# Second expert layer: two of eight token tiles through all eight experts instead of sorted blocks

## The reference, cut to what matters

```python
logits = xt @ Wg.T                                   # 1024 x 8
topk_logits, topk_idx = jax.lax.top_k(logits, TOP_K) # TOP_K = 2
w = jax.nn.softmax(topk_logits, axis=-1)
gates = jnp.zeros((T, N_EXPERTS), xt.dtype).at[rows, topk_idx].add(w)
h = jnp.einsum('th,ehi->tei', xt, W1) + b1           # 128 -> 512 for each expert
h = jax.nn.gelu(h, approximate=False)
o = jnp.einsum('tei,eih->teh', h, W2) + b2           # 512 -> 128
y = jnp.einsum('te,teh->th', gates, o)
x = _layernorm(x + y)
```

## Time and profile before

| | |
|---|---|
| median of 3 runs | 872.15 us (870.58 to 873.14) |
| the profiled execution | 871.81 us, of which the span in the profile is 870.0 us |
| mean granted clock of PE | 0.863 of full |
| PE busy | 706.4 us (81%) |
| DVE busy | 587.0 us (67%) |
| ACT busy | 452.8 us (52%) |
| POOL busy | 441.5 us (51%) |

### The profile page before, as it was taken

How to read it: one execution, slowest core, us unless ns; L and a number is a source line. 1 busy time by engine, 2 the same in 40 slices (tenths; PEclk the granted TensorE clock), 3 DMA queues, 4 the chain that set the end, 5 groups by cost and what they waited for, 6 DMA issues and landing times.

```text
span 870.0 us, 21282 instructions
## 1 busy us (share of the span) xinstructions
PE 706.4 (81%) x7894; PEld 524.7 (60%) x7894; DVE 587.0 (67%) x1552; ACT 452.8 (52%) x1155; POOL 441.5 (51%) x595
## 2 busy tenths in 40 slices
PE   5997987899989996999958998649968999733990
PEld 2575754667867784777526776316545667532980
DVE  4657859899889865798478987403348889541544
ACT  2214646677887654777516764304426767311660
POOL 3119835676656632443246874124556667342452
PEclk9658978899999998999978998659969999755995
DMA  8009200000000000000038000030026570003012
GB/s 325 5 9 293 35 2 1 1 1 2 2 1 1 2 2 1 3 3 3 2 12 280 3 3 2 4 91 32 35 67 182 168 210 3 3 28 92 32 37 76
DMA packets 50803, 44.66 MB, mean 51 GB/s; under 512 B 15408, under 2 KB 41136, under 8 KB 50192
## 3 DMA queue, kind: packets, MB, share of 16 engines
q1 hardware_dynamic: 48464, 38.70, 16.0%
q0 software_dynamic: 2240, 4.60, 1.5%
HBM read 30.94 MB, written 12.36 MB: 50 GB/s over the span
## 4 chain that ended last, share of the span: by engine, by line
PE 48%; DVE 16%; issue 16%; POOL 6%; ACT 5%; DMA 5%; SPq 2%; DVEq 0%; POOLq 0%; ACTq 0%
PE bank L830 4%; PE bank L809 4%; PE bank L818 3%; PE bank L989 3%; PE bank L1062 3%; PE bank L1055 2%; PE bank L727 2%; PE bank L899 2%; PE bank L845 2%; DMA rel_scratch<-G 2%; DVE pairs L1570 2%; DVE pairs L1566 2%; PE bank L876 2%; PE bank L720 1%; PE bank L740 1%
## 5 line engine op out<-in xcount | busy, mean ns | idle before, releaser
L1880 POOL TENSOR_TENSOR sm<-sm,mx 128x512 f32<-128x512 f32 x80 | 83.8, 1049 | 41.9 <-DVE mx L1520 41.3
L1851 POOL TENSOR_SCALAR veps<-mv 128x1 f32<-128x1 f32 x112 | 26.9, 240 | 117.7 <-DVE mv L1455 117.5
L1153 ACT COPY pT<-bank 128x512 f32<-128x512 f32 x112 | 65.4, 584 | 36.4 <-PE bank L818 35.0
L1148 ACT ACTIVATE pr<-sm 128x512 f32<-128x512 f32 x112 | 70.1, 632 | 25.4 <-POOL sm L1880 24.6
L818 PE MATMUL bank<-W,pr 128*128 128x128 f32 x448 | 71.6, 283 | 7.5 <-ACT pT L1153 6.0
L1875 POOL TENSOR_TENSOR pairs<-KS,quad 128x512 f32<-128x512 f32 x56 | 59.9, 1071 | 35.1 <-ACT KS L1130 35.0
L1852 POOL TENSOR_TENSOR rstd<-veps,W 128x1 f32<-128x1 f32 x112 | 65.1, 581 | 9.3
L830 PEld LDWEIGHTS bank<-VX,pT 64*64 64x64 f32 x3584 | 60.2, 139 | 13.5 <-issue 7.6
L809 PE MATMUL bank<-pairs,Q 64*128 64x256 f32 x448 | 66.3, 415 | 2.0 <-DVE sm L1505 1.0
L830 PE MATMUL bank<-VX,pT 64*64 64x9 f32 (+1 forms) x3584 | 65.4, 203 | 2.9 <-ACT pT L1153 1.2
L818 PEld LDWEIGHTS bank<-W,pr 128*128 128x128 f32 x448 | 50.4, 143 | 19.4 <-issue 10.9
(11 more groups left out here) (344 smaller groups left out, 1909.5 us busy)
## 6 DMA issues: line engine op xcount, KB each, us to landing
big<-gup SPq DMA_DIRECT2D x4, 1024.0 KB, 10.0
rel_scratch<-G SPq DMA_DIRECT2D x16, 256.0 KB, 2.8
W<-small SPq DMA_DIRECT2D x1, 3206.5 KB, 12.4
big<-early SPq DMA_DIRECT2D x2, 1557.0 KB, 8.3
slots_x<-zero SPq DMA_DIRECT2D x2, 1472.0 KB, 25.1
big<-down SPq DMA_DIRECT2D x8, 256.0 KB, 8.5
QM<-rel_scratch SPq DMA_DIRECT2D x16, 128.0 KB, 2.7
PM<-rel_scratch SPq DMA_DIRECT2D x16, 128.0 KB, 2.7
```

The lines of the kernel that those rows point to most:

```text
L1148: act.activation(pr[:, u % 2, 4 * h:4 * h + 4, :, :].rearrange("p g b k -> p b g k"), sm[:, 2 * (u % 2) + h, :].rearrange("p (b g k) -> p ...
L1153: act.copy(pT[:, u % 2, 4 * h:4 * h + 4, :], bank[BK[f"tu{h}"]][:, :].rearrange("p (h n) -> p h n", h=4)).then_inc(pt_ready, 1)
L1880: tt(v, v, bc(mx[:, slot, :], [P, 8, S], 2), ALU.subtract).then_inc(pcentered, 1)
```

## The change

Tiles 0 to 5 (`SORTED` = 6) stay sorted: `BLOCKS3` = (1536 + 1016)/128 = 19 blocks, 12 scatters instead of 16. Tiles 6 and 7 go through all eight experts, 256 columns wide, with zero gates for those that a token didn't choose. This dense stage stands between the routing and the block loop in the queues of PE, ACT and DVE.

The logits of tiles 0 to 5 are issued in the chain, ahead of the turn of tile 6; those of tiles 6 and 7 follow behind the rank products. The choice of the two experts (`choose_two`) is made twice on the DVE, first for tiles 0 to 5, and for the others behind the slots. On PE `all_up(e)` multiplies with W1 in four chunks into banks 4 and 5, `all_down(e - 1)` with W2 into banks 2 and 3; the gates are turned and the bias is multiplied behind expert 1's `all_down`. On ACT the Exp of the gates stands between the GELUs of experts 0 and 1. On the DVE the additions of the eight experts and the statistics of tiles 6 and 7 stand ahead of the `value_load`s (now 19), their normalisation behind the bias copy. SP sends tiles 6 and 7 out ahead of its wait for the results. In the tail the two halves are of three tiles each.

The core of the diff:

```diff
-BLOCKS3 = (2 * TOK + NE3 * (P - 1)) // P
+SORTED = 6
+BLOCKS3 = (2 * SORTED * P + NE3 * (P - 1)) // P
...
+        HD = [G[:, 2 * i:2 * i + 2, :].rearrange("p a n -> p (a n)").rearrange("p (c n) -> p c n", c=4) for i in range(2)]
...
-            sp.wait_ge(scattered, 16 * MT * 3)
+            sp.wait_ge(scattered, 16 * (MT + 2 * SORTED))
             slots_in(slots3_x, BLOCKS3)
+
+            def output(t, done):
+                sp.wait_ge(x_ready, LAST_NORM - MT + done)
+                sp.dma_start(out[:, t:t + 1, :], X[:, t:t + 1, :]).then_inc(out_sent, 16)
+
+            for t in range(SORTED, MT):
+                output(t, t - SORTED + 1)
...
+                        if name == "x3" and t == SORTED:
+                            logits("e3.r", NE3, range(SORTED))
...
             def top2_ffn():
-                logits("e3.r", NE3)
...
+                logits("e3.r", NE3, range(SORTED, MT))
+                wide = (MT - SORTED) * P
+
+                def all_up(e):
+                    if e == 0:
+                        pe.wait_ge(e3_in, 16 * 12)
+                    for c in range(4):
+                        mm(fill(4 + c % 2, h3_ready)[:, 0:wide], tile(e3_w[:, e, :], c), XT[:, SORTED * P:], start=True,
+                           stop=True).then_inc(h3_full, 1)
+
+                def all_down(e):
+                    pe.wait_ge(h3_ready, 4 * e + 4)
+                    ps = fill(2 + e % 2, row_added)
+                    for t in range(MT - SORTED):
+                        for c in range(4):
+                            last = mm(tile(ps, t), tile(HD[e % 2][:, c, :], t), tile(e3_w[:, e, :], 4 + c), start=(c == 0), stop=(c == 3))
+                    last.then_inc(block_full, 1)
+
+                def gate_rows():
+                    pe.wait_ge(one_ready, 5)
+                    for hh in range(2):
+                        ps = fill(hh, choice_ready)
+                        for t in range(NT):
+                            last = pe.transpose(ps[0:NE3, t * P:(t + 1) * P], gate[:, NT * hh + t, 0:NE3], ident)
+                        last.then_inc(choice_full, 1)
+
+                def second_bias():
+                    for hh in range(2):
+                        pe.wait_ge(choice_ready, hh + 1)
+                        ps = fill(hh, acc_ready)
+                        for t in range(NT):
+                            last = mm(tile(ps, t), tile(gT, NT * hh + t), w("e3.b2")[0:NE3, :], start=True, stop=True)
+                        last.then_inc(b2_full, 1)
+
+                for e in range(NE3 + 1):
+                    if e < NE3:
+                        all_up(e)
+                    if e >= 1:
+                        all_down(e - 1)
+                    if e == 2:
+                        gate_rows()
+                        second_bias()
...
+                def all_gelus(e):
+                    for c in range(4):
+                        if e >= 2 and c == 0:
+                            act.wait_ge(block_full, BLOCKS + e - 1)
+                        act.wait_ge(h3_full, 4 * e + c + 1)
+                        act.activation(HD[e % 2][:, c, :], bank[4 + c % 2][:, 0:(MT - SORTED) * P], ACT.Gelu,
+                                       bias=w("e3.b1", 4 * e + c, 4 * e + c + 1)).then_inc(h3_ready, 1)
+
+                for t in range(SORTED):
                     act.copy(XB[:, t, :], X[:, t, :]).then_inc(xs_ready, 1)
-                act.wait_ge(lg_ready, 3)
-                act.activation(col[:, 4, :], col[:, 3, :], ACT.Exp).then_inc(score_ready, 1)
-                for t in range(MT):
+                for t in range(SORTED):
                     act.copy(XK[:, t, 0:P], X[:, t, :]).then_inc(xs_ready, 1)
-                for hh in range(2):
-                    act.wait_ge(choice_full, hh + 1)
-                    act.copy(half(gT, hh), bank[hh][0:NE3, :]).then_inc(choice_ready, 1)
+                for e in range(NE3):
+                    all_gelus(e)
+                    if e == 0:
+                        act.wait_ge(lg_ready, 4)
+                        act.activation(col[:, 4, :], col[:, 3, :], ACT.Exp).then_inc(score_ready, 1)
+                    if e == 2:
+                        for hh in range(2):
+                            act.wait_ge(choice_full, hh + 1)
+                            act.copy(half(gT, hh), bank[hh][0:NE3, :]).then_inc(choice_ready, 1)
...
+            def choose_two(tiles, n):
+                dve.wait_ge(logit_full, 1 + n)
+                l8, one8, two8 = lg[:, tiles, 0:NE3], one[:, tiles, 0:NE3], one[:, tiles, NE3:2 * NE3]
+                dve.tensor_copy(l8, bank[6][:, tiles.start * NE3:tiles.stop * NE3].rearrange("p (t e) -> p t e", e=NE3)).then_inc(
+                    lg_ready, 1)
+                dve.wait_ge(lg_ready, 1 + n)
+                link(choose_first(one8, l8, NE3, w("down8"), tiles))
+                link(dve.tensor_copy(col[:, 2, tiles], col[:, 0, tiles]))
+                link(stt(l8, one8, -BIG, l8, ALU.mult, ALU.add))
+                choose_first(two8, l8, NE3, w("down8"), tiles).then_inc(one_ready, 1)
+                dve.wait_ge(one_ready, 2 + n)
+                return tt(col[:, 3, tiles], col[:, 0, tiles], col[:, 2, tiles], ALU.subtract)
+
             def top2_ffn():
-                dve.wait_ge(logit_full, 2)
-                l8, g8, one8, two8 = lg[:, :, 0:NE3], gate[:, :, 0:NE3], one[:, :, 0:NE3], one[:, :, NE3:2 * NE3]
-                dve.tensor_copy(l8, bank[6][:, 0:MT * NE3].rearrange("p (t e) -> p t e", t=MT)).then_inc(lg_ready, 1)
-                dve.wait_ge(lg_ready, 2)
-                link(choose_first(one8, l8, NE3, w("down8")))
-                link(dve.tensor_copy(col[:, 2, :], col[:, 0, :]))
-                link(stt(l8, one8, -BIG, l8, ALU.mult, ALU.add))
-                choose_first(two8, l8, NE3, w("down8")).then_inc(one_ready, 1)
-                dve.wait_ge(one_ready, 3)
-                tt(col[:, 3, :], col[:, 0, :], col[:, 2, :], ALU.subtract).then_inc(lg_ready, 1)
-                dve.memset(newrow[:, 1:NE2:2, 0:1], 1.0).then_inc(init_dve, 1)
-                ts(XK[:, :, P].bitcast(I32), XB_id[:, :, P].bitcast(I32), float(TOK + BLOCKS * P), None, ALU.add).then_inc(init_dve, 1)
+                link(choose_two(slice(0, SORTED), 1))
...
+                choose_two(slice(SORTED, MT), 2).then_inc(lg_ready, 1)
...
+                rest = range(SORTED, MT)
+                dve.wait_ge(acc_ready, 2)
+                for e in range(NE3):
+                    dve.wait_ge(block_full, BLOCKS + e + 1)
+                    if e >= 1:
+                        dve.wait_ge(row_added, e)
+                    for t in rest:
+                        last = stt(total_y[:, t, :], tile(bank[2 + e % 2], t - SORTED), gate[:, t, e:e + 1], total_y[:, t, :], ALU.mult,
+                                   ALU.add)
+                    last.then_inc(row_added, 1)
+                dve.wait_ge(row_added, NE3)
+                for t in rest:
+                    own_norm_done(t)
+                    stats(total_y[:, t, :], t)
                 dve.wait_ge(slot_ready, 4)
                 start = [dve.value_load(owner[0:1, j:j + 1], min_val=0, max_val=(NE3 - 1) * WIDE3) for j in range(BLOCKS3)]
                 dve.wait_ge(e3_in, 16 * 12)
                 link(dve.tensor_copy(e3_w[:, :, 2 * NF3:WIDE3], w("e3.b1").rearrange("p (e c) -> p e c", e=NE3)))
 
+                for t in rest:
+                    dve.wait_ge(rstd_ready, due(rstd_ready))
+                    finish(total_y[:, t, :], t)
+
                 def fetch(j):
                     if j >= 3:
-                        dve.wait_ge(block_full, BLOCKS + j - 2)
+                        dve.wait_ge(block_full, BLOCKS + NE3 + j - 2)
...
+                def finish_rows(hh):
+                    for t in range(SORTED // 2 * hh, SORTED // 2 * (hh + 1)):
                         dve.wait_ge(rstd_ready, due(rstd_ready))
-                        finish(total_y[:, NT + t, :], NT + t)
+                        finish(total_y[:, t, :], t, t // 4 * 4)
+
+                for hh in range(2):
+                    for k in range(2):
+                        add_rows(hh, k)
+                    if hh == 1:
+                        finish_rows(0)
+                    for t in range(SORTED // 2 * hh, SORTED // 2 * (hh + 1)):
+                        own_norm_done(t, t // 4 * 4)
+                        stats(total_y[:, t, :], t, t // 4 * 4)
+                finish_rows(1)
...
-            for m in range(2 * MT):
-                rows = XB_id if m < MT else XK
+            for m in range(2 * SORTED):
+                rows = XB_id if m < SORTED else XK
                 pool.wait_ge(xs_ready, MT + m + 1)
-                pool.indirect_dma_start(slots3_x, bass.IndirectOffsetOnAxis(ap=slot3[:, m:m + 1], axis=0), rows[:, m % MT, :],
+                pool.indirect_dma_start(slots3_x, bass.IndirectOffsetOnAxis(ap=slot3[:, m:m + 1], axis=0), rows[:, m % SORTED, :],
```

(16 more changed lines are left out.)

94 lines of the change are left out of this document (40 added, 54 removed).

## The result

The changed kernel took 882.86 us (median of 4 runs, 878.26 to 885.15) against 871.69 us of the kernel before beside it: ratio 1.0128, 95% interval 1.0081 to 1.0176. It is slower by 1.3%; the forecast was 887.8 us, 876 to 895. The profiled execution took 882.33 us, its span is 880.5.

A forecast was written before the change was run, and what follows sets the result against it. PE bounds the expert blocks; 23 serial value_loads on the DVE, not the rows, release the first block. First block +26.5 us, four blocks -7.6, tail -3.0 make +15.9 on 871.81: 887.8 us, range 876 to 895.

The forecast's parts named there:

- Step 1: Routing: logits of tiles 0 to 5 start earlier, 12 scatters instead of 16; first block's rows land 9.7 us sooner.
- Step 3: Dense stage's start: table loads around ACT's Exp make PE wait within expert 1, from 769.0 to 772.0.
- Step 4: Clock in the dense stage: PE rises to full clock at 780.5, 8.5 us after 772.
- Step 5: Rest of the dense stage: remaining up and down parts, gate transposes and bias products; PE ends at 806.6.
- Step 6: DVE behind the dense stage: additions, statistics, then 19 loads at 0.727 us, 13.8 us uncovered; first block at 823.85.
- Step 7: Block loop: starts at half clock, four blocks fewer at 1.89 us each, 41.8 us instead of 49.4.
- Step 8: Tail: four additions and two tiles' statistics and normalisation less; 3.0 us saved.
- Step 2: Dense stage on PE: one expert of 256 columns costs 3.9 us at full clock, all eight 31 us.
- Rival 5: PE stays at half clock through the dense stage because two banks make it wait; about 911 us, chance 0.05.
- rival 2: Loads are cheaper than in their row because POOL's scatters no longer run beside them; 882.6 us, chance 0.15.
- rival 3: Loads are cheap, 4.3 us in all, and most of the old gap was something else; 878.3 us, chance 0.07.
- Rival 4: Loads cost next to nothing and blocks start at 810.0 at full clock; 869.5 us or 864.8, chance 0.08.

The follow-up runs named there:

- e10: Changed kernel with seven tiles sorted, the 21 loads, bias copy and first fetches spread over the DVE's idle spots, Exp behind expert 1; 870.94 us, ratio 0.9991 to the kernel before.
- e4: Changed kernel without any value_load: block owners are fixed numbers, reading the owners left out; 876.8 us in one run, 117.7 us from the last output projection's start to the end.
- e5: Changed kernel with loads, bias copy and first three fetches ahead of the dense additions, later normalisation of tiles 6 and 7, Exp behind expert 1; 870.93 us, ratio 0.9984.
- e3: Kernel before with its 23 value_loads moved ahead of the bias additions; 870.20 us, ratio 1.0061 to the kernel before unaltered.
- e7: As e5 but with seven tiles sorted, 21 blocks, 14 scatters and one dense tile 128 columns wide; 870.43 us, ratio 0.9993 to the kernel before.
- c1: The changed kernel run again, unaltered; 885.35 us, ratio 1.0175 to the kernel before.
- e6: As e5, but the Exp of the gates stays behind the GELUs of expert 0; 866.32 us, ratio 0.9961 to the kernel before.
- e9: As e5 with six tiles sorted, but the 19 loads, bias copy and first fetches spread over the DVE's idle spots; 868.53 us, ratio 0.9975 to the kernel before.
- e1: Changed kernel with its 19 value_loads moved behind the gates of the second choice, ahead of the bias terms; 878.23 us, ratio 1.0119 to the kernel before.
- e8: The same program as e1, run a second time; 864.05 us in a single run.
- e11: The same program as e1, run a third time with more executions; 880.15 us over 6 runs, ratio 1.0121 to the kernel before.
- e2: Changed kernel with ACT's Exp of the gates behind the GELUs of expert 1 instead of expert 0; 887.19 us, ratio 1.0213 to the kernel before.

## Why the prediction was right, and where its sizes were off

The profiled layers ahead of the entry were 2.28 us shorter than before. With that added, the rows stand beside the steps so:

| step | forecast | measured, moved by 2.28 |
|---|---|---|
| 1 logits start | 756.0 | 755.9 |
| 1 first and last scatter | 766.4, 780.4 | 766.5, 780.5 |
| 3 PE waits for the Exp | 3.0 us | 3.11 us |
| 4 clock rises | 780.5 | 777.6, with a dip from 784.4 to 787.8 |
| 5 dense stage ends | 806.6 | 807.8 |
| 6 statistics end | 808.2 | 809.4 |
| 6 loads | 13.8 us | 12.12 us |
| 6 first block | 823.9 | 823.1 |
| 7 blocks | 41.8 us | 39.96 us |
| 8 tail | 3.0 us less | 3.5 us less |

**Steps 1 and 3** held to 0.1 us in the rows above; PE's wait for the Exp lay 0.3 us sooner. Since they are moved DVE and POOL chains with their durations from the rows of before, there was little to miss.

**Step 2**, one expert at 3.9 us, measured 3.97 (787.65 to 791.62). A product of 256 columns lasts 1.03 us for four instructions; the value between the two bounds, taken in proportion to the columns, was the right choice.

**Step 4** put the clock's rise 3 us late, which is 1.5 us of PE's time, and a dip of 3.4 us that it did not have gave that back: that the end of the stage came out near is in part luck. Rival 5, half clock throughout, did not happen here; e10 had it through much of its dense stage.

**Step 6** carried the sign of the result and is shown by e4: the hole is the loads. Its price was 0.638 us instead of 0.727. If a load costs that in the old kernel too, its gap of 16.73 us held 2.1 us of something else (23 x 0.638 = 14.7); no run took the loads out of that kernel. That is rival 2's direction but not its reason: the loads cost the same 0.63 us beside running scatters (e5: 11.97 us for 19) as without them. The 0.2 us for a register from HBM (the Trainium skill, "Runtime: NRT & Kernel Launch", Instruction fetch mechanics) would have made 3.8 us; these loads from SBUF were three times as dear, so the page's figure can't be carried over to them, and rivals 3 and 4 fell with it. The wait of PE behind the DVE's queue was as described.

**Step 7** was mis-sized by 1.8 us: I let the clock rise after 8.9 us, as I read it in the profile before (9.1 by its stretches), and it rose after 5.7. One profile does not give that time: in e3, the kernel before with its loads moved, it was 4.0. The four blocks themselves are 7.6 us (two blocks more make 3.8 us between e5 and e7).

**Step 8** was 0.5 us short.

**The sum.** Aligned, first block +25.75, blocks -9.44, tail -3.52: +12.8 us against +15.9 forecast. The 3.1 us between them: loads 1.7, the way from them to the first product 0.3, blocks 1.8 and tail 0.5 were cheaper, the dense stage 1.2 dearer. The remaining 2.28 us to the measured +10.5 come from layers that the change does not touch, whose end differs by several us from one execution to the next. c1 gives +13.4 from the entry.

**Rival 4** named where the gain would lie, and e6 shows the state it describes. The Trainium skill ("TensorE: Matmul & The Clock Gate", Part 1) says that the half clock is the default and activity releases it, so blocks right behind dense work would begin at full clock; the trace agrees in e5, e6 and e9, where PE idled 0.35 us and the blocks took 37.5 us. "Right behind" is meant strictly: behind 4.08 us of idle time, in e1, e4, e8 and e11, the clock was up when the blocks began, fell to 1.2 GHz 0.1 to 0.8 us after and came back 3.4 us later, which made the blocks 1.3 us longer. Its first block at 810.0 is 55.1 us after the entry, and e6 measured 54.9. That is in part luck: e6 has a wait of 2.27 us for the DVE that the rival did not have, and its clock rose 20 us after the entry and not 25.6. And the rival stood on cheap loads, and they are dear: what made it true was to put them where nobody waits for the DVE.

**What stays open.** The standstills of ACT, and in e3 of the DVE, are not explained. They begin in the stretch of the indirect scatters, no engine is named for them, and packets that load instructions lie at none of them. Those of e1, e2, e3 and e11 end 0.01 to 0.7 us after SP issues the reload, so at about the time when the scatters have landed; those of e9 and the main one of e10 end before it. A kernel without scatters was not tried. They are a part of what e9 and e10 missed their forecasts by (6 and 12 us; in e10 the loads are another), and the best version found, e6, beats the kernel before by only 0.4% (interval 0.0 to 0.8%), hardly more than can be told from nothing.

## What to carry to other kernels

Work that is invisible in the profile because it has no row (register loads, here 0.64 us each) is priced from the gap that holds it, and the question for each move is what runs beside it: the same loads cost about 1 us beside a wait for rows, 12 us behind a dense stage, and 2 to 10 us where the DVE has banks to empty. A change that fills one engine's wait also takes the cover from another engine's. A gap marked "issue" can still hold a wait for another engine: in e10 it was found by laying the rows of DVE and ACT side by side. And a moved wait is judged by more than one execution: the one of e8 showed 15 us gained behind the entry, while the ten others of the same program fit half of that.

## What the runs showed of the hardware

- A `value_load` from SBUF into DVE registers took 0.638 us (12.12 us for 19, twice), 0.623 to 0.630 in e6 and e5 (11.84 and 11.97 us), 0.641 for 21 in e7, with or without scatters beside it. In small groups the gap does not follow that price: 3.01 and 2.96 us for four in e9 and e10, 1.33 and 1.60 for three behind an addition.
- In stretches with indirect scatters an engine can stand still for 3 to 7 us without a named releaser: ACT in e1, e2, e9, e10 and e11; by the price of its loads the DVE for some 5 us in e3 (and 2 us in the kernel before); and PE for 1.4 us in c1 and e4. It repeats for one program (e1 and e11 at the same place to 0.1 us), and was absent once (e8).
- The clock rose 5.7 us after the first block matmul in the changed kernel, 6.3 in c1, 9.1 in the kernel before and 4.0 in e3, in the same block loop. A pause of 4.08 us was paid for after it, not in it: granted 1.00 up to 804 us in e8, 0.56 and 0.59 in the two stretches of 2 us after the blocks had begun at 803.68, 1.00 again from 808.
- The untouched layers ahead of the last projection ended between 749.0 and 762.8 us in 14 profiles, more than most of the effects studied here.
